# Packed cross-attention in a two-layer transformer: where the head merges, the gathers and the later maxima stand

## What is computed

```python
def _attention(xq, xkv, wq, wk, wv, wo, bo):
    B, S, _ = xq.shape
    T = xkv.shape[1]                      # 77 context tokens
    q = (xq @ wq).reshape(B, S, N_HEADS, D_HEAD)
    k = (xkv @ wk).reshape(B, T, N_HEADS, D_HEAD)
    v = (xkv @ wv).reshape(B, T, N_HEADS, D_HEAD)
    scale = D_HEAD ** (-0.5)
    attn = jnp.einsum('bihd,bjhd->bhij', q, k) * scale
    attn = jax.nn.softmax(attn, axis=-1)
    out = jnp.einsum('bhij,bjhd->bihd', attn, v).reshape(B, S, D_ATTN)
    return out @ wo + bo
...
x = x + attention(layer_norm(x), layer_norm(x), ...)   # self
x = x + attention(layer_norm(x), context, ...)         # cross
x = x + geglu(layer_norm(x))                           # feed-forward
```

## Time and profile before

| | us |
|---|---|
| median of 3 runs | 2564.97 |
| lowest and highest of them | 2563.12, 2571.70 |
| the profiled execution, device time | 2564.95 |
| span of its instructions | 2563.2 |

### The profile page before, as it was taken

One profiled execution on the slowest core, in us unless ns is written; L12 is line 12 of the kernel. 1 busy time (PEld: TensorE's weight loads), 2 busy tenths in 40 slices (PEclk: granted clock), 3 DMA queues, 4 the chain that ended last, 5 costly groups with the idle time before them and its releaser, 6 DMA issues.

```text
span 2563.2 us, 59118 instructions
## 1 busy us (share of the span) xinstructions
PE 2234.4 (87%) x25392; PEld 1483.4 (58%) x25392; DVE 1760.3 (69%) x3148; ACT 1475.6 (58%) x1948; POOL 1165.7 (45%) x730
## 2 busy tenths in 40 slices
PE   4999998879699999878959999988797999998788
PEld 1566666565366666656525666665653666666565
DVE  6888884545588888454548888845456888885454
ACT  2887885324288888432327888853243888884232
POOL 3667663212176666321216666632122676652311
PEclk8999999889799999888969999999897999999889
DMA  3312210000131221000023122100002223110000
GB/s 80 84 47 73 65 45 18 9 9 15 32 84 47 76 63 45 18 9 10 15 64 79 52 69 70 45 18 9 10 15 49 66 55 84 47 33 18 18 1 17
DMA packets 52437, 106.62 MB, mean 42 GB/s; under 512 B 9552, under 2 KB 13648, under 8 KB 52176
## 3 DMA queue, kind: packets, MB, share of 16 engines
q1 hardware_dynamic: 52176, 102.84, 15.1%
HBM read 50.25 MB, written 2.10 MB: 20 GB/s over the span
## 4 chain that ended last, share of the span: by engine, by line
PE 62%; DVE 19%; ACT 11%; issue 4%; DMA 2%; POOL 1%; SPq 1%; POOLq 0%; DVEq 0%; ACTq 0%
PE scores L688 7%; PE scores L689 7%; PE scores L690 7%; PE work L769 6%; PE scores L796 6%; PE scores L789 6%; DVE minima L1299 6%; DVE prob L1314 3%; PE work L688 3%; PE work L690 3%; PE work L689 3%; ACT prob L1120 3%; PE work L818 3%; PE work L814 3%; PE work L816 3%
## 5 line engine op out<-in xcount | busy, mean ns | idle before, releaser
L636 POOL TENSOR_TENSOR prob<-prob 128x1024 f16<-128x1024 f32 x256 | 582.5, 2275 | 557.1 <-ACT prob L1121 546.4
L1299 DVE TENSOR_REDUCE minima<-work 128x1 f32<-128x512 f32 x1024 | 681.3, 683 | 52.5 <-PE work L769 36.2
L1120 ACT ACTIVATE prob<-scores 128x1024 f32<-128x1024 f32 x512 | 526.0, 1027 | 125.9 <-PE scores L796 109.1
L1121 ACT ACTIVATE prob<-scores 128x1024 f16<-128x1024 f32 x512 | 522.9, 1021 | 0.0
L814 PE MATMUL work<-vals,prob 128*128 128x65 f16 x4096 | 429.7, 193 | 15.4 <-POOL prob L636 13.3
L818 PE MATMUL work<-vals,prob 128*128 128x65 f16 x4096 | 430.3, 195 | 0.0
L816 PE MATMUL work<-vals,prob 128*128 128x64 f16 x4096 | 430.2, 193 | 0.0
L814 PEld LDWEIGHTS work<-vals,prob 128*128 128x128 f16 x4096 | 383.5, 99 | 77.9 <-POOL prob L636 15.1
L769 PE MATMUL work<-ka,qa 128*128 128x512 f16 x1024 | 401.8, 396 | 24.9 <-DMA kb<-staged_k 15.7
L816 PEld LDWEIGHTS work<-vals,prob 128*128 128x128 f16 x4096 | 380.5, 97 | 58.1
L818 PEld LDWEIGHTS work<-vals,prob 128*128 128x128 f16 x4096 | 381.0, 97 | 0.0
(11 more groups left out here) (166 smaller groups left out, 4593.4 us busy)
## 6 DMA issues: line engine op xcount, KB each, us to landing
qa<-staged_q SPq DMA_DIRECT2D x128, 128.0 KB, 2.4
ka<-staged_k SPq DMA_DIRECT2D x128, 128.0 KB, 2.4
raw_even<-in_pairs SPq DMA_DIRECT2D x32, 384.0 KB, 3.4
raw_odd<-in_pairs SPq DMA_DIRECT2D x32, 384.0 KB, 3.3
raw_odd<-in_pieces SPq DMA_DIRECT2D x20, 512.0 KB, 3.5
raw_even<-in_pieces SPq DMA_DIRECT2D x20, 512.0 KB, 3.7
qb<-staged_q SPq DMA_DIRECT2D x64, 128.0 KB, 2.4
kb<-staged_k SPq DMA_DIRECT2D x64, 128.0 KB, 2.4
```

Of the source, the lines that this page charges most:

```text
L636: pool.tensor_tensor(prob[1][:, slot, :], prob32[:, slot, :], prob[0][:, slot, :], ALU.subtract).then_inc(a.polished, 1)
L1120: act.activation(prob32[:, n % RING, :], source, ACT.Exp)
L1121: act.activation(prob[0][:, n % RING, :], source, ACT.Exp)\
L1299: dve.tensor_reduce(minima[:, t, h:h + 1], out[:, :], AX.X, ALU.max, negate=True)\
```

## The change

Five things change, all in `cross`. No arithmetic is added or removed.

1. On TensorE the merges of step n stand inside `score(n)`, between its quarters: behind the second quarter and behind the fourth (in step 3 behind the third).
2. On ScalarE the merge copies of step n stand ahead of the exponentials of step n.
3. On VectorE `refine(n-1)` comes first, then all merges of step n, then the gathers.
4. The gathers wait head by head on a new semaphore, `xheads_full`, in place of waiting for the half step in which the head ended.
5. The twelve later maxima stand beside steps 0 to 2, one behind each quarter, and `shift(1)` stands behind the first quarter of `score(3)`.

```diff
 def x_merges(n):
     if n < 3:
-        return [], []
+        return []
     block, d = divmod(n - 3, X_STEPS)
-    pairs = [(block, p) for p in x_pairs(d)]
-    return pairs[:1], pairs[1:]
...
+    return [(block, p) for p in x_pairs(d)]
+
+X_LATER = [(HALF + t, g) for t in range(HALF) for g in range(len(PEAK_GROUPS))]
...
@@ TensorE, score
-                def score(n, between):
+                def score(n, beside):
...
-                        if i < len(between):
-                            peak(*between[i])
+                            if 2 * i + c in beside:
+                                step, at_ = beside[2 * i + c]
+                                step(*at_)
@@ TensorE, value
+                            if ends:
+                                last.then_inc(xheads_full, 1)
+                    if not ends:
                         last.then_inc(xprobs_used, 1)
@@ TensorE, the steps
                 for n in range(X_ALL):
-                    before, after = x_merges(n)
-                    peaks = x_peaks(n)
-                    score(n, peaks[:2])
-                    for m in before:
-                        merge(*m)
+                    beside = {}
+                    if n < 3:
+                        beside = {k: (peak, at) for k, at in enumerate(X_LATER[4 * n:4 * n + 4])}
+                    elif n == 3:
+                        beside[0] = shift, (1,)
+                    for k, m in zip((2, 3) if n == 3 else (1, 3), x_merges(n)):
+                        beside[k] = merge, m
+                    score(n, beside)
                     if n >= X_LAG:
                         value(n - X_LAG)
-                    for at in peaks[2:]:
-                        peak(*at)
-                    if n == 4:
-                        shift(1)
-                    for m in after:
-                        merge(*m)
@@ ScalarE
                     if n >= X_RING:
-                        act.wait_ge(xprobs_used, 2 * (g * X_ALL + n + 1 - X_RING))
+                        heads, steps = x_used(n - X_RING)
+                        if (n - X_RING) % X_STEPS == X_STEPS - 1:
+                            act.wait_ge(xheads_full, g * BLKS * HEADS + heads)
+                        else:
+                            act.wait_ge(xprobs_used, g * BLKS * (X_STEPS - 1) + steps)
...
                 for n in range(X_ALL + X_LAG + 1):
+                    for m in x_merges(n):
+                        merge(*m)
                     if n < X_ALL:
                         exponential(n)
-                    for m in sum(x_merges(n), []):
-                        merge(*m)
@@ VectorE
-                    for i, h in [(i, h) for i in range(2) for _, h, _, ends in x_parts(2 * d + i) if ends]:
-                        dve.wait_ge(xprobs_used, 2 * (g * X_ALL + n) + i + 1)
+                    for h in x_ended(d):
                         seq = block_ * HEADS + h
+                        dve.wait_ge(xheads_full, g * BLKS * HEADS + seq + 1)
...
                 for n in range(X_ALL):
-                    before, after = x_merges(n)
-                    peaks = x_peaks(n)
-                    for at in peaks[:2]:
-                        peak(*at)
-                    for m in before:
-                        merge(*m)
+                    if n < 3:
+                        for at in X_LATER[4 * n:4 * n + 4]:
+                            peak(*at)
+                    elif n == 3:
+                        shift(1)
                     if n and not x_by_pool(n - 1):
                         refine(n - 1)
+                    for m in x_merges(n):
+                        merge(*m)
                     if n >= X_LAG:
                         gather(n - X_LAG)
-                    for at in peaks[2:]:
-                        peak(*at)
-                    if n == 4:
-                        shift(1)
-                    for m in after:
-                        merge(*m)
...
-                merge(1, 3)
-                refine(X_ALL - 1)
+                refine(X_ALL - 1)
+                merge(1, 3)
```

More of the change, by code:

```diff
@@ L89, in x_by_pool, with x_used @@
     return n in (1, 3, 6, 8)
+def x_used(n):
+    block, d = divmod(n, X_STEPS)
+    return (block * HEADS + sum(len(x_ended(k)) for k in range(d + 1)), block * (X_STEPS - 1) + d + 1)
 def x_lows(n):
@@ L99, in x_merges @@
     if n < 3:
-        return [], []
+        return []
     block, d = divmod(n - 3, X_STEPS)
-    pairs = [(block, p) for p in x_pairs(d)]
-    return pairs[:1], pairs[1:]
[L106 to L113, removed]
+    return [(block, p) for p in x_pairs(d)]
+X_MERGES = [(b, p) for b in range(BLKS) for p in range(PAIRS)]
+X_LATER = [(HALF + t, g) for t in range(HALF) for g in range(len(PEAK_GROUPS))]
 Step = collections.namedtuple("Step", "kind step par head ahead")
@@ L425, in build @@
         xprobs_used = sem("xprobs_used")
+        xheads_full = sem("xheads_full")
         xinverse = sem("xinverse")
```

## The result

The changed kernel takes 2434.51 us (median of four runs, 2430.97 to 2436.33); the kernel before, run beside it, 2567.97 (2563.12 to 2571.7). The ratio is 0.948, interval 0.9457 to 0.9502. The forecast was 2438. The profiled execution took 2436.33, its span 2434.6.

What follows compares the result with a forecast made beforehand. TensorE bounds the kernel, losing time to gather waits and a low clock. Per round 69.9 work + 7.7 stalls + 0.4 gives 78 us against 109.7, saving 127 of 2564.95: 2438 us, own range 2424 to 2456, 8-in-10 range 2414 to 2474.

Steps and rivals of the forecast that it cites:

- Stalls left: TensorE's remaining waits a round: 1.2 double steps, 1.8 value pieces, 2.8 peaks, 1.9 tail; 7.7 us, none over 1.1.
- 69.9: Pure TensorE work of a round at full clock, in us: scores, value, merges, projections, later peaks and shift(1).
- second merge in the score: Both merges of a step share one bank, so 0.3 us is left in each of four double steps: 1.2.
- the second peak of step 0: VectorE is in two subtractions until 463.02, so the first maximum is read late: about 1.0 us stall.
- the tail: End of a round: value(8) and value(9) wait about 1.0 and 0.7 us for gathers, first merge 0.2: 1.9.
- value pieces: In steps 4, 6, 7 and 9 the value's last piece waits 0.3 to 0.6 us for gathers: 1.8 in all.
- the check on the round before: Account of a round before the change: 69.9 + 24.3 idle + 14 for the clock = 108.2, against 109.7 us measured.
- 2.8 of round trips: Later peaks wait on the trip through x_high: nine times 0.2, plus 1.0 at step 0; together 2.8 us a round.
- rival 1: TensorE's clock stays low in part, so 10 us a round come back: 2478 us; chance 0.08.
- rival 2: Three refines a round blocked behind GpSimd, each by up to 4.5 us; TensorE feels 7.5 a round: 2468; chance 0.11.
- rival 3: Slower than before: refine, merges, copy and exponentials become one ring at the second merge in the score: 2605 us; chance 0.02.
- rival 4: The wait merely moves from value to merges because VectorE is the real limit: within 0.3% of 2565 us; chance 0.02.

## Why the prediction was right

**The mechanism.** It held in the steps whose rows stand above. The gather stood behind a refine and two exponentials that it did not need; both orders alone, with TensorE untouched, win 86% of the stretches' gain. The waits for gathers were to fall to about 15 us, the longest to about 1; they fell to 7.9 on the matmuls and 11.3 on the weight loads, none above 0.8. Steps 4 to 9 of the first round take 5.3 to 6.4 us each in the timeline, near what was put (5 to 6.3).

**The sum.** Stretches of 78 us a round were forecast, 78.3 came. The gain in them was put at 127 and is 125.5. The span came out 3.1 shorter outside them, which nobody had forecast and which is scatter.

**Stalls left.** The sum was right: 78.3 - 69.9 = 8.4 us a round, where 7.7 + 0.4 was put. A shown wait is short by the 0.17 by which a matmul's modelled end runs past its slot, which was in the account of before. With it a second merge in the score waits 0.34 (0.3 was put), the second peak of step 0 waits 0.93 (1.0), and the tail 0.81 and 0.66 (1.0 and 0.7). Two of the four value pieces wait 0.6 (0.3 to 0.6), the other two so little that only the weight loads show it. From one later peak to the next, 476.81 - 475.66 = 1.15 us go where 0.98 was the work, a stall of 0.17 for which no wait shows. The others cost from nothing (the two that follow a shift) to 0.36, and the ten behind the second peak together 1.8, as put. That is also why TensorE's busy time is 74.2 a round and not the 71 that was put: short stalls lie under modelled ends and count as busy, and of each longer one so does 0.17. As a mark for the result 71 was wrong; 78 was right.

**The clock.** It was to be at full level because no gap over 1.1 us is left, and was granted 1.00. Its price before was put at 14 us a round, half of the 28 at the low level, "if TensorE is busy there throughout". It is 11.2 by the busy time of before and after, and 10.6 by the unused matmuls. The trace of before has the condition itself. These are all its stretches with a clock of 0.50 in the four rounds, 25 of them, in sum:

```profile
sum 112.68, PE 100.98 PEld 67.06 DVE 45.38 ACT 9.83 POOL 21.36; mean PE 4.04 PEld 2.68 DVE 1.82 ACT 0.39 POOL 0.85
```

That is 28.2 us a round, as put, with TensorE busy for 25.2 of them. The 3.0 us of idle take 1.5 off the 14 and leave 12.6. Another part is that the value's matmuls are less than twice as fast at the full level: the twelve of a piece took 540.92 - 540.28 = 0.64 at the low level, and take 0.37 at the full one.

```profile
540.28 0.23 PE L943 MATMUL work<-xv,prob 124*128 124x65 f16 x1 [3.95 <-DVE o_nat L1400]
...
540.92 0.67 PE L688 MATMUL scores<-hT,wide 128*124 128x512 f16 x1
```

What the rest of the difference is stays open. The forecast did not suffer, as it was built up from the work and not by taking the loss off. But the check on the round before closed by two errors that met: with 11.2 for the clock, 69.9 + 24.3 + 11.2 = 105.4, and 4.3 are left for modelled ends, not the 1.7 of ten gaps. After the change the same remainder, 74.2 - 69.9, is 4.3 too.

**What it did not see.** Three of the six refines in each round of before stood behind a polish: 2.15 us for 1.21. The prediction named the rule, but only for blocks that the change might bring. It took the 2.06 of the earlier trace rows as the refine's own time and VectorE's 49.3 us as fixed. The change ends all three: VectorE is busy for 46.4 a round, and each of the 24 refines takes 1.20 to 1.22.

**The edits' prices.** Edit 4 was bounded at plus or minus 1; it wins 1.7, so the bound was too narrow. It hides "in the above", as put, only in so far as those stalls had been worked out with it. Edit 5 was said to buy that steps 3 and 4 hold no peak any more; on the kernel before it buys nothing and costs 0.7 a round. Its 2.8 of round trips less the 0.7 paid before is 2.1, so by the difference, an estimate, some 1.4 does come back, yet not enough; no row shows where. Edit 1's own worth was not in the prediction; it is 3.7.

**The rivals.** The clock staying low in part (rival 1) did not come. The kernel before shows a clock that swings (0.86 to 0.89) with waits of up to 4.0 us. The Trainium skill's case (TensorE: Matmul & The Clock Gate, "A second HAM failure mode") is of very short gaps between groups of matmuls that alone keep the clock swinging; with gaps of 0.8 us or less no run here shows it. Blocked refines (rival 2) are real, as the run with GpSimd's bias sum held back shows, but missed the changed kernel by 0.3 us, and the one that was made costs 1.7 us a round and not the 2.5 put. The Trainium skill's rule that the later of the two fully blocks (SBUF — State Buffer, "Who interferes with whom") agrees with the trace: 3.86 us for a refine that takes 1.20 alone. `refine(4)` and `refine(7)` did not meet the splits. A slower ring (rival 3) and a wait that merely moves (rival 4) have no row for them: new waits at the merges are 0.17.

**What stays open.** What part of edit 5's cost in the whole change comes back through steps 3 and 4 was not run on the changed kernel.

## What to carry to other kernels

When the tensor engine waits long for a small operation, follow the chain back through the queues and ask of each instruction in it whether the next one needs it or merely stands behind it: two such places, a copy behind two exponentials and a merge ahead of a refine, held 27 of 31 us a round here, and to swap them cost nothing. Moving the waiter's own work so as to cover the wait won 3.7 more. Where such waits lower the clock, price that too: here 24.3 us of idle a round cost 10.6 to 11.2 more. And do not add up what single edits win: apart the two swaps win 11.6 and 21.0, together 26.9, since the clock and the blocked refines can be won back only once.

## What was not expected of the hardware

- Matmuls whose result nothing reads, in gaps of up to 4 us, made the whole kernel faster: 80 more a round and 10.6 us less, the clock from 0.87 to 1.00.
- The clock came back before the waits were gone: 0.98 with waits of up to 1.6 us (42.2 in all), 1.00 with the same longest wait and 25.1 in all, but 0.91 with 2.3 and 56.1.
- A blocked refine ends 1.08 us after GpSimd's instruction, whether that had 1.1 us left to run (a polish) or 2.8 (the bias sum): a little less than the 1.20 that it takes alone.
- The block goes the other way as well. In the kernel before, GpSimd's instruction behind the polish of the earlier trace rows started at 482.87, just as the blocked refine (481.83 to 483.98) was let through, and took 2.02 us; in the changed kernel, where no refine is beside it, it takes 1.04. Two of these stand in every round. With them GpSimd's busy time fell from 24.1 to 22.2 us a round.

```profile
482.87 2.02 POOL L585 TENSOR_SCALAR wide<-raw_even 128x1024 f16<-128x1024 f32 x1
```

```profile
487.90 1.04 POOL L586 TENSOR_SCALAR wide<-raw_even 128x1024 f16<-128x1024 f32 x1
```
